# Routing of a mixture-of-experts layer moved into the attention ahead of it

## The reference

```python
x = L0_attn_hidden_states                      # (16, 256, 128) float32
x = x + _layernorm(_L0_attn_ref(_layernorm(x), ...))   # two rounds of attention, 16 heads of 8
x = x + _layernorm(_L0_ffn_ref(_layernorm(x), ...))    # 8 experts, top 2, and a shared expert
x = x + _layernorm(_L1_attn_ref(_layernorm(x), ...))
x = x + _layernorm(_L1_ffn_ref(_layernorm(x), ...))

def _L0_ffn_ref(x, shared_w1, shared_w2, experts_w1, experts_w2, gate_w):
    shared = silu(x_flat @ shared_w1.T) @ shared_w2.T
    gate_logits = x_flat @ gate_w.T                    # (4096, 8)
    top_k_gates, top_k_idx = jax.lax.top_k(gate_logits, 2)
    top_k_gates = jax.nn.softmax(top_k_gates, axis=1)
    ...
    return (shared + selected).reshape(B, S, D)        # each token: its 2 experts, weighted
```

## Time and profile before

| what | us |
|---|---|
| median of 3 runs | 1840.53 |
| the runs | 1840.53, 1835.14, 1918.26 |
| the profiled execution | 1829.01 |
| its span, first to last instruction | 1827.1 |
| of it, first attention | 0 to 596.4 |
| first feed-forward | 596.9 to 887 |
| both second stages | 888 to 1827.1 |

### The profile page before, as it was taken

The page is one execution under the profiler, slowest core; times in us unless marked ns, Lnnn a source line. Parts: engine busy times, 40 slices in busy tenths (PEclk is TensorE's granted clock), DMA queues, the critical chain, the costliest instruction groups (busy, mean ns, idle before and its releaser), DMA issues. The chain is left out here.

```text
span 1827.1 us, 38589 instructions
## 1 busy us (share of the span) xinstructions
PE 1536.2 (84%) x12053; PEld 1164.6 (64%) x12053; DVE 1178.4 (64%) x3204; ACT 1020.5 (56%) x1873; POOL 779.0 (43%) x999
## 2 busy tenths in 40 slices
PE   2599999999996974899349998988888999689997
PEld 1466666666664853898226666666666666478886
DVE  2366777777665441899646776766767766556676
ACT  1388777777874251777205555655555666444332
POOL 7765554646511077899663333333333212101111
PEclk9999999999999586999758999999999999889999
DMA  5121000000000011222211111111111111000000
GB/s 187 52 71 44 19 18 14 17 16 17 18 16 1 1 42 51 67 71 71 79 35 35 34 33 33 35 34 33 33 31 33 29 30 31 6 1 6 11 6 24
DMA packets 81602, 63.33 MB, mean 35 GB/s; under 512 B 17472, under 2 KB 77632, under 8 KB 81088
## 3 DMA queue, kind: packets, MB, share of 16 engines
q1 hardware_dynamic: 77376, 53.36, 10.0%
q0 software_dynamic: 4096, 8.40, 1.5%
HBM read 20.01 MB, written 16.52 MB: 20 GB/s over the span
## 5 line engine op out<-in xcount | busy, mean ns | idle before, releaser
L1116 DVE TENSOR_REDUCE a_qt<-a_ps_m 128x2 fp32r<-128x512 f32 (+1 forms) x384 | 264.9, 690 | 160.0 <-PE a_ps_m L902 112.2
L408 ACT ACTIVATE a_p<-a_ps_s 128x1024 f32<-128x1024 f32 x256 | 264.3, 1034 | 37.8 <-PE a_ps_s L286 34.3
L511 DVE TENSOR_REDUCE a_qt<-a_ps_m 128x2 fp32r<-128x512 f32 x256 | 176.6, 690 | 85.6 <-PE a_ps_m L297 83.7
L652 POOL TENSOR_TENSOR a_rn<-a_ss,a_half 128x16 f32<-128x16 f32 x64 | 185.9, 2914 | 2.2 <-POOL a_ss L670 1.5
L902 PE MATMUL a_ps_m<-a_kpad,a_qs 128*128 128x512 f32 x256 | 129.5, 506 | 51.1 <-DVE a_qt L1116 47.6
L1029 ACT ACTIVATE a_pg<-a_ps_s 128x1024 f32<-128x1024 f32 x128 | 131.8, 1030 | 17.4 <-PE a_ps_s L877 12.0
L304 PE MATMUL a_ps_o<-a_p,a_v 128*32 128x256 f32 x2048 | 137.5, 386 | 2.0 <-ACT a_p L408 1.5
L297 PE MATMUL a_ps_m<-a_kpad,a_qs 128*128 128x512 f32 x256 | 117.9, 460 | 13.8 <-DVE a_qt L511 11.4
L902 PEld LDWEIGHTS a_ps_m<-a_kpad,a_qs 128*128 128x128 f32 x256 | 49.5, 193 | 101.8 <-DVE a_qt L1116 84.9
L1347 POOL COPY a_v<-a_vt 128x64 f32<-128x64 f32 x64 | 15.4, 241 | 222.1 <-PE a_ps_o L979 222.1
L868 PE MATMUL a_ps_a<-ident,a_qt 128*128 128x128 f32 x512 | 108.6, 295 | 1.6 <-ACT a_ks L1023 1.2
(11 more groups left out here) (336 smaller groups left out, 4339.6 us busy)
## 6 DMA issues: line engine op xcount, KB each, us to landing
a_kpad<-a_ks SPq DMA_DIRECT2D x768, 32.0 KB, 1.8
xs<-a_zero SPq DMA_DIRECT2D x39, 128.0 KB, 2.1
f_xin<-xs SPq DMA_DIRECT2D x39, 128.0 KB, 2.1
ys<-f_yout SPq DMA_DIRECT2D x39, 128.0 KB, 1.9
w<-in_w SPq DMA_DIRECT2D x2, 2304.0 KB, 11.3
out_x<-X SPq DMA_DIRECT2D x8, 256.0 KB, 2.3
wgu<-in_wgu SPq DMA_DIRECT2D x1, 1152.0 KB, 5.0
xs<-Z,rows POOLq DMA_INDIRECT x64, 2.2
```

What stands on the lines that cost most here:

```text
L408: nc.scalar.activation(probs[:, u % 2, 2 * c:2 * c + 2, :, :].rearrange("p a b c -> p (a b c)"), ps_s[:, n % 2, :], ACT.Exp).then_inc(exp_ ...
L511: nc.vector.tensor_reduce(qt2[:, k % 2, 2 * part:2 * part + 2, SHIFT], ps_m[:, :, :], AX.X, ALU.max, negate=True).then_inc(max_done, 1)
L652: nc.gpsimd.tensor_tensor(rn[:, part * c:(part + 1) * c], ss[:, part * c:(part + 1) * c], half[:, 0:c], ALU.pow).then_inc(rn_ready, 1)
L1116: nc.vector.tensor_reduce(dst, src, AX.X, ALU.max, negate=True).then_inc(max_done, 1)
```

## The change

The gate's logits, the choice of experts and the placement move into the first attention for batches 0 to 13, in groups of batches 0 to 3, 4 to 7, 8 to 11 and 12 to 13; batches 14 and 15 stay in the feed-forward. Each expert has a fixed region of 4352 rows in xs, so a group's rows are known once it is placed (`taken` carries each expert's count on). Per step:

- in steps 4b+3, for batch b-3: two transposes of Z (`zT`), behind O1 on TensorE, copied by ScalarE behind Q;
- in steps 4b, for batch b-4: two products with the gate (`lg`) in plain float32, copied by VectorE;
- VectorE's choice of a group: 5, 4 and 3 instructions in steps 29 to 31, 45 to 47, 61 to 63 and 69 to 71, ahead of maxima 3; `place` on TensorE (9 products, 5 for the last group) in steps 32, 48, 64, 72; 4 and 5 instructions of VectorE in that step and the next;
- GpSimd's scatters of the first three groups, two at the end of each of steps 34 to 41, 50 to 57 and 66 to 73. Those of the group of batches 12 to 13 (8) come first thing in the feed-forward, those of batches 14 and 15 (8) after their routing.

The loop of the attention is written out. The zero fills of all xs are replaced by 7 fills of spare slots and one at the end of each expert's region, at an address from a register; the loads of slots take their address from a register too. XH and XL hold two blocks and are computed as the shared expert goes, the last block first; the shared result is copied straight into Z except that block's.

```diff
+REGION = B * S + SLOT_T
+SPARE = SLOTS - 2 * B * S // SLOT_T
+GROUPS = ((0, 3), (4, 7), (8, 11), (12, 13), (14, 15))
+ROUTED = GROUPS[-2][1] + 1
+PLACE_STEP = 8
...
-    LOOP = (2, B // 2 - 2)
...
+    A_ORDER = ("T1", "T2", "K", "xT", "yT", "Q", "zT")
+    B_ORDER = ("qp", "kp", "vp", "O2", "op", "O1", "lg", "place")
...
+        for k in range(FIRST, LAST):
             yield Step(k)
...
-                if 0 <= k < 13:
-                    for n in range(3 * k, 3 * k + 3):
-                        sp.dma_start(a["xs"][n * SLOT_T:(n + 1) * SLOT_T, :].rearrange("(t p) d -> p t d", p=P),
-                                     zero[:, :, :]).then_inc(filled, 16)
...
+                if a_live(k, "zT"):
+                    pe.wait_ge(z_new, b - 2)
+                    wait_a(st, "zT")
+                    transposes(ps_a, lambda t: Z[:, ((b - 3) * TPB + t) * D:((b - 3) * TPB + t + 1) * D], a_full)
+                if b_live(k, "lg"):
+                    pe.wait_ge(a["later"], 16 * a["laters"])
+                    pe.wait_ge(a_done, a_count(k - 1, "zT"))
+                    wait_b(st, "lg")
+                    for t in range(TPB):
+                        last = nc.tensor.matmul(ps_b[:, t * EXPERTS:(t + 1) * EXPERTS], zT[:, t * P:(t + 1) * P],
+                                                rt["gate"][:, :], start=True, stop=True)
+                    last.then_inc(b_full, 1)
+                g = places(k)
+                if g is not None:
+                    pe.wait_ge(route, ROUTE_SET_UP + ROUTE_LINKS * g + CHOSEN)
+                    wait_b(st, "place")
+                    place_tokens(nc, ps_b, rt, GROUPS[g]).then_inc(b_full, 1)
                 if unit(k - 3):
                     score_chunk(st, 3, qs2m[:, :])
                 maxima(st, 3)
...
+                if b_live(k, "lg"):
+                    dve.wait_ge(b_full, b_count(k, "lg"))
...
+                for g, (first, last) in enumerate(GROUPS[:-1]):
+                    part = k - (NG * (last + 3) + PLACE_STEP)
...
+                    if -3 <= part < 0:
+                        choose(nc, link, rt, GROUPS[g], part + 3)
+                    if 0 <= part < 2:
+                        if part == 0:
+                            dve.wait_ge(b_full, b_count(k, "place"))
+                        place(nc, link, rt, GROUPS[g], ps_b, part, b_done)
                 maxima(3)
...
+                for g, (first, last) in enumerate(GROUPS[:-2]):
+                    part = k - (NG * (last + 3) + PLACE_STEP + 2)
+                    if part == 0:
+                        pool.wait_ge(route, ROUTE_SET_UP + ROUTE_LINKS * (g + 1))
+                    if 0 <= part < 8:
+                        scatter(nc, Z, rt, first * TPB + part, a["xs"], a["scattered"])
...
+            for e in range(E):
+                at = nc.sync.value_load(pad_at[0:1, e:e + 1], min_val=e * REGION, max_val=e * REGION + B * S)
+                sp.dma_start(a["xs"][bass.ds(at, SLOT_T), :].rearrange("(t p) d -> p t d", p=P),
+                             zero[:, :, :]).then_inc(padded, 16)
...
+            take_x(0)
+            logits()
+            pe.wait_ge(w_hi, 2)
+            pe.wait_ge(w_lo, 2)
+            take_x(1)
+            up(0)
+            for n in range(1, NT + 2):
                 if n + 1 < NT:
-                    route(n + 1)
...
+                    take_x(n + 1)
                 if n < NT:
                     up(n)
-                back(n - 2)
+                if n == 1:
+                    pe.wait_ge(routed, LOGITS + CHOSEN)
+                    place_tokens(nc, ps_l, rt, GROUPS[-1]).then_inc(routing_full, 1)
+                if n >= 2:
+                    back(n - 2)
                 if n - 1 < NT:
                     down(n - 1)
...
                         nc.scalar.activation(s[:, part(c2)], ps_u[:, c2, :], ACT.Silu).then_inc(silu_done, 1)
+                    if n + 2 < NT:
+                        split_x(n + 2)
                     for c2 in range(2):
                         act.wait_ge(silu_done, 2 * n + c2 + 1)
                         wait(act, y_full, n)
...
+            pool.wait_ge(scattered, EARLY)
+            for i in range(GROUPS[-2][0] * TPB, GROUPS[-1][0] * TPB):
+                scatter(nc, Z, rt, i, a["xs"], scattered)
+            pool.wait_ge(routed, AT)
+            for i in range(GROUPS[-1][0] * TPB, TILES):
+                scatter(nc, Z, rt, i, a["xs"], scattered)
```

More of the change, by code:

```diff
@@ L108, in steps, with places @@
     def steps(eng):
[L109 removed]
+        for k in range(FIRST, LAST):
             yield Step(k)
[L111 to L115 removed]
+    def places(k):
+        for g, (first, last) in enumerate(GROUPS[:-1]):
+            if k == NG * (last + 3) + PLACE_STEP:
+                return g
+        return None
@@ L1577, in up, with take_x, logits @@
-            def up(n):
+            def take_x(n):
+                wait(pe, xl_ready, n)
+                i = ORDER[n] * TT
+                transposes(ps_x, lambda t: Z[:, (i + t) * D:(i + t + 1) * D], TT, x_full)
+            def logits():
+                pe.wait_ge(routed, LOGITS - 1)
+                pe.wait_ge(xl_ready, 1)
+                for t in range(TT):
+                    tok, dst = slice(t * P, (t + 1) * P), ps_l[:, t * E:(t + 1) * E]
+                    nc.tensor.matmul(dst, XH[:, 0, tok], gwh[:, :], start=True, stop=False)
+                    nc.tensor.matmul(dst, XH[:, 0, tok], gwl[:, :], start=False, stop=False)
+                    last = nc.tensor.matmul(dst, XL[:, 0, tok], gwh[:, :], start=False, stop=True)
+                last.then_inc(routing_full, 1)
@@ L1756, in split_s @@
+            split_x(1)
             def split_s(n):
@@ L1785, in _ @@
+            split_s(0)
+            dve.wait_ge(routing_full, PLACED)
+            for step in range(2):
+                place(nc, link, rt, GROUPS[-1], ps_l, step, tables)
+            full = [P, SLOTS, E]
+            link(nc.vector.tensor_tensor(cnt[:, :], rt["taken"][:, :], rt["start"], ALU.subtract))
+            link(nc.vector.tensor_tensor(ge[:, :, :], cnt[:, :].unsqueeze(2).to_broadcast([P, E, 16]),
                                          fill.unsqueeze(1).to_broadcast([P, E, 16]), ALU.is_gt))
-            link(nc.vector.tensor_reduce(nt[:, :], ge, AX.X, ALU.add))
@@ L1791, in _ @@
-            link(nc.vector.scalar_tensor_tensor(
-                out=far, in0=base[:, :].unsqueeze(1).to_broadcast(full), scalar=float(SLOT_T),
-                in1=ps_l[:, 0:width].rearrange("p (t e) -> p t e", e=E), op0=ALU.mult, op1=ALU.add))
-            for n, sel in enumerate((sel1, sel2)):
-                link(nc.vector.tensor_tensor(key, sel[:, :, :], far, ALU.mult))
-                link(nc.vector.tensor_reduce(fpos[:, :], key, AX.X, ALU.add))
-                last = nc.vector.tensor_copy(a["rows"][:].rearrange("p (b k t) -> p b k t", k=2, t=TPB)[:, :, n, :],
-                                             fpos[:, :].rearrange("p (b t) -> p b t", t=TPB))
-                link(last)
```

403 lines of the change are left out of this document (232 added, 171 removed).

## The result

The kernel after takes 1851.89 us in the median of four runs (1849.62 to 1854.06), the kernel before 1837.84 in four beside them. One of those four, at 1918.26, ran in the chip's slower state and is left out of the ratio. The ratio is 1.0084, with a 95% interval of 1.0055 to 1.0114: less than the 2% that counts as a change, but the interval lies wholly above 1, so the kernel is some 0.8% slower. Forecast were 1850 us and a net of +10. The profiled execution after is 1849.62 us (span 1847.4, before 1827.1).

A forecast was written before the change was run, and what follows sets the result against it. TensorE was taken to bound the first attention (busy 443.6 of 460 us), late routing and scatters the feed-forward. Attention +45.5 and feed-forward -35.4 net +10 on 1829.0, 1839; with the median 11.5 above, 1850; range 1812 to 1880.

The forecast's parts named there:

- zT, steps 15 to 59: First attention, steps 4b+3: TensorE waits for ScalarE's copy of Q before zT; 1.15 us, 12 times, +13.8 us.
- lg, steps 16 to 60: First attention, steps 4b: TensorE waits for VectorE's read of O1 before lg; 1.6 us, 12 times, +19.2 us.
- slack taken back: First attention: 0.2 us deducted for each of the 24 zT and lg charges, for unplaced slack; -4.8 us.
- placement, steps 32, 48, 64: First attention: place stands behind lg, waits for VectorE's copy, then runs 9 products; 1.4 us, three times, +4.2 us.
- VectorE's choice, steps 29, 33, 45, 49: First attention: five instructions delay the scaling of q and k; 1.0 us in four steps, +4.0 us, between 0 and 5.
- scatters, steps 35 to 54: First attention: GpSimd's scatters between the norms' powers in steps 36, 40, 52; 0.8 us each, +2.4 us, between 0 and 7.8.
- drain and hand-over: End of the first attention: the last group's scatters delay the rstd chain and outlive VectorE; +9.1 us, bounds 3 and 12.
- Rival A: First attention: zT, lg and the rest cost only their floors, being absorbed; net -18 us, 1823 us; chance 0.22.
- Rival B: First attention: more idle stretches lower TensorE's clock; at 0.94 it costs +31 us, giving 1881 us; chance 0.12.
- The feed-forward: From its start to the first slot: earlier routing and fewer late scatters gain 35.4 us, bounds 45 and 23.
- cast 1: Feed-forward: ScalarE's second cast of the hidden values, put 25 us after the stage's start S, against S+42.6 before.
- Rival C: Feed-forward: the shared stage stays at half clock, taking 12 us off the gain; 1862 us; chance 0.16.

The follow-up runs named there:

- unrolled: Kernel before with only the first attention's loop written out; ratio 0.9994 against the kernel before, feed-forward starting at 592.72 us against 596.97.
- lg_early: Kernel after with the lg products and VectorE's copy moved to the output projection's place, behind O2; next stage 5.5 us earlier, total time not given.
- tail_out: Kernel after with the third group's 16 scatters moved from the attention to the start of the feed-forward; 1873.99 us, ratio 1.0155 against the kernel before.
- scatters_out: Kernel after with no scatter in the attention, all 64 issued in the feed-forward; 1835.71 us, ratio 1.0033 against the kernel before.
- the control: Kernel before, unchanged, run again to see where the second stages' extra time comes from; its second stages took 936.3 us.
- zt_early: Kernel after with zT's transposes and ScalarE's copy moved ahead of Q, behind K's copy; next stage 9.8 us earlier, total time not given.
- place_early: Kernel after with the placement's products moved to the output projection's place in steps 33, 49, 65; ratio 1.0062 against the kernel before.
- best2: Kernel after with zT, lg and placement earlier, all scatters out of the attention, ScalarE's copy behind the casts, second attention's loop written out; 1777.34 us, ratio 0.9713.

## Why the forecast time was right, and where its steps were wrong

The base is the run unrolled. The numbers are differences of step lengths, in us; "start of step 15" is what the kernels differ by until then:

```
term                                       forecast   measured
zT, steps 15 to 59                            +13.8     +13.7  (1.16 each, 0.85 in step 59)
lg, steps 16 to 60                            +19.2     +20.5  (1.71 each)
slack taken back                               -4.8        0
placement, steps 32, 48, 64                    +4.2      +6.8  (1.49, 2.77, 2.52)
lg and zT at 63, 64, 67                        +2.1      +1.9
VectorE's choice, steps 29, 33, 45, 49         +4.0        0   (-0.01, +0.06, -0.02, -0.02)
scatters, steps 35 to 54                       +2.4      +3.1  (0.9 in 38 and 42, 0.2 to 0.3 in five)
other steps from 53 on                           0       +0.9
unrolling                                      -4.5      -4.3
drain and hand-over                            +9.1     +12.7  (9.35 scatters, 1.65 choice, 1.75 hand-over)
start of step 15                                 0       -1.0
sum                                           +45.5     +54.3
```

- **zT and lg** held to 0.1 us each, mechanism included: with the place, they lost the wait and kept the issue. What failed is "for slack that I can't place I take back 0.2 for each of the 24": the steps show none, and the sum had no reason for the term. Rival A's floor of 0.25 for zT is what zT pays once moved (0.22); for lg 0.5 was too low (0.82).
- **VectorE's +4.0**: the step said that the scaling of q and k loses its wait for GpSimd once lg has made the step before longer, so that the five instructions of the choice would delay it. It does not lose it. In step 26, without a choice, the scaling still waits 1.43 us; in step 30, behind the five instructions, no wait is left, and it starts at the same point of the step (0.90 us in). The choice fills the wait, and the steps are not longer, in any run.

```profile
275.20 0.69 DVE L658 TENSOR_TENSOR a_scaled<-a_qk,a_rn 128x512 f32<-128x512 f32 x1 [1.43 <-POOL a_rn L789]
...
309.50 0.69 DVE L658 TENSOR_TENSOR a_scaled<-a_qk,a_rn 128x512 f32<-128x512 f32 x1
```

- **GpSimd's scatters** between the powers (steps 36, 40, 52): forecast were 0.8 us three times. Steps 38 and 42 are 0.9 us longer, step 54 only 0.06, and five other steps 0.2 to 0.3. The reason given, that lg's 1.7 us cover most of the 2.6, fits lg_early: with less of that cover steps 38, 42 and 54 cost 3.5, 3.8 and 1.2 us, together a little over the bound of 7.8, part of it by the clock.
- **The placement** was mis-sized: +4.2 against +6.8. Each stands where TensorE has waited twice. In steps 48 and 64 the clock then falls to its lower level for some 4 us, and they cost 2.8 and 2.5 us; in step 32 it stays up, and that one costs 1.5, as forecast. Rival B spoke of the clock over the whole stage, where it stayed near 1.00; the fall is local. In other runs step 32 costs up to 2.8 us more, with a longer fall.
- **The drain**: the scatters' +9.1 were right (9.35 by tail_out), at 0.95 to 1.14 us each. That they might take half as much again beside VectorE did not come there. By the Trainium skill's rule ("SBUF — State Buffer", "Who interferes with whom") a subtraction of two SBUF operands should not hold them up, and two scatters beside such a one (f_sl, at 674.97 and 676.24) took 0.955 us: there the trace agrees. The five of the drain that took 1.09 to 1.14 us all ran beside a tensor_scalar of VectorE (L593). The one long wait of VectorE was 4.55 us, where about 7 was forecast. Two things were not in the sum: the choice and placement of the last group on VectorE, between the output projection and its norm (1.65 us, by scatters_out), and the hand-over after indirect transfers (1.75 us).
- **The feed-forward** gained 43.7, not 35.4, and near the upper bound of 45. Routing ahead of the first up projection was right to 0.1 us. Too dear were cast 1 (S+25 against S+22.7) and +1.5 for each of the casts 2 to 5: the intervals from there on are 9.08, 10.48, 9.06, 10.66, 9.82 and 9.79, with more clock than before. Rival C (half clock) did not come: 0.86.
- **The second stages** were taken as unchanged, silently. They cost +9.6 in the two profiles, and +7 between the control and the changed kernels beside it.
- **The sum**: the attention missed by +8.8 us, the feed-forward by -8.3 and the second stages by +9.6, so two of the three cancel and the net is +20, not +10. That the time is still within 2 us of 1850 is luck. The sum was put on a median of three that lay 11.5 us above its profiled execution; after, the median lies 2.3 us above.

So the 43.7 us that were won are given back. zT and lg charge 34 us, of which 22 are waits on two single PSUM buffers (by zt_early and lg_early) and the rest their issue. The placement beside them charges 7, scatters where nothing could hide them 12, the last group's choice and the hand-over 3.4, and the second stages 7 to 10.

## What to carry to other kernels

Work that is moved into an idle-looking stage is paid by what stands in order behind it: put it where the shared buffer has just been read, and the price falls to its issue (1.16 to 0.22 us here, 1.71 to 0.82). Before a gain is taken for granted look at what else the moved work lengthened, for the wait of one engine can be the cover of another. And compare a step at a loop's back-edge with the same step in straight code: here that view was worth 28 us, more than any other edit.

## What was not expected of the hardware

- A hardware loop costs 1.1 us per round in the first attention (4.25 over four), but 4.4 to 6.9 us at each back-edge in the second. And this changes with kernels that differ only elsewhere: by +0.4 to +2.2 us per round against the control. Why was not tested. That it hangs on where the loop's code comes to lie is only a guess.
- A block in which GpSimd issued indirect transfers ends late: 0.53 us from VectorE's last instruction to the next stage without any, 2.28 with the last scatter 87 us before, 3.2 with it 8.7 us before, and 4.25 from the end of GpSimd's last scatter when that comes last.
- Behind a stand-still of about 1 us, a second of 0.36 and nine small products TensorE's clock goes from 1.00 to 0.55 for some 4 us in step 48 of the kernel after, and not in step 32, where the same comes ahead. The same products without the stand-stills left it at 1.00 six times of six (place_early, best2).
- In three of the runs measured together ScalarE stood up to 24.5 us in the feed-forward (15 of them with its operands there), with nothing on this core that ended the wait. It came while GpSimd issued scatters, in the kernel before with its loop written out too, and not in later profiles with the same scatters.
